# Batch loop of a two-layer mega-kernel written out: order of the batches, place of the experts, one projection run, and the shifted value rows by DMA from ScalarE's queue

## What is computed

```
x0  = x[b]                                  # (512, 128)
xn0 = layernorm(x0)
g   = minGRU(xn0) @ W2 + b2                 # log-space recurrence over tokens, width 256
h   = xn0
for l in 0, 1:                              # local attention, 8 heads of 64, window 64
    s = shift_token(h)                      # upper half of the channels one token later
    q, k, v = s @ wqkv[l]                   # q, k normalised, rotated
    h = h + local_softmax(q, k) @ v @ wo[l]
    h = h + mlp(layernorm(shift_token(h)))  # gelu gate, hidden 341
x1  = silu(h) * g + x0
xn1 = layernorm(x1)
o   = softmax(q1 k1^T, 16 heads of 16) v1 (heads of 64) @ wo1
out[b] = x1 + gate * o                      # gate: silu of the expert layer's result
```

## Time and profile before

| | |
|---|---|
| median of 3 runs | 3997.4 us (3994.64 to 4002.34) |
| the profiled execution's own time | 3996.54 us |
| its span (first to last instruction) | 3994.5 us |
| PE busy | 3230.1 us, 81% |
| DVE busy | 2735.6 us, 68% |
| ACT busy | 2412.9 us, 60% |
| POOL busy | 980.4 us, 25% |
| mean granted PE clock | 0.907 |

### The profile page before, as it was taken

One profiled execution on the slowest core, in us unless ns is written; L12 is line 12 of the kernel. 1 busy time (PEld: TensorE's weight loads), 2 busy tenths in 40 slices (PEclk: granted clock), 3 DMA queues, 4 the chain that ended last, 5 costly groups with the idle time before them and its releaser, 6 DMA issues.

```text
span 3994.5 us, 66851 instructions
## 1 busy us (share of the span) xinstructions
PE 3230.1 (81%) x20144; PEld 1629.3 (41%) x20144; DVE 2735.6 (68%) x4828; ACT 2412.9 (60%) x5081; POOL 980.4 (25%) x719
## 2 busy tenths in 40 slices
PE   4768788787878879787888878787887878788866
PEld 2445344444434444443434444343444444343411
DVE  3464486777767676777767677777767777786632
ACT  2344466666756666566766656675666667576543
POOL 1121121323222122322222132322212232232110
PEclk7679899898989989899998989999998989999876
DMA  2002001010010101001010101001010100101010
GB/s 65 1 4 67 20 20 49 19 49 15 16 51 20 47 20 47 13 30 37 21 47 20 47 20 41 19 20 51 19 48 16 51 13 23 44 17 47 20 50 19
DMA packets 112590, 124.19 MB, mean 31 GB/s; under 512 B 12435, under 2 KB 85693, under 8 KB 112189
## 3 DMA queue, kind: packets, MB, share of 16 engines
q1 hardware_dynamic: 112124, 119.26, 9.3%
q0 software_dynamic: 64, 0.01, 0.0%
HBM read 64.70 MB, written 54.53 MB: 30 GB/s over the span
## 4 chain that ended last, share of the span: by engine, by line
PE 55%; DVE 19%; issue 14%; ACT 6%; POOL 4%; DVEq 1%; SPq 1%; DMA 0%; POOLq 0%; ACTq 0%
PE pb L569 29%; PE o_bank L569 10%; PE s L569 7%; DVE nmax L1285 3%; PE y_bank L569 3%; PE pb L664 3%; PE pb L695 2%; POOL scratch L1370 2%; DVE stat L1179 2%; ACT ex L1017 2%; DVE stat L1209 2%; DVE scratch L1191 1%; PE pb L719 1%; DVE scratch L1192 1%; DVE mlp_h L1253 1%
## 5 line engine op out<-in xcount | busy, mean ns | idle before, releaser
L1017 ACT ACTIVATE ex<-s,nmax 128x512 f32<-128x512 f32 x1024 | 698.2, 684 | 510.4 <-DVE nmax L1285 485.2
L1285 DVE TENSOR_REDUCE nmax<-s 128x1 f32<-128x512 f32 x1024 | 684.4, 684 | 388.4 <-PE s L569 386.9
L1404 POOL TENSOR_TENSOR vsc<-vrow,rinv 128x256 f32<-128x256 f32 x256 | 172.9, 675 | 1755.0 <-DVE rinv L1293 1748.1
L569 PE MATMUL o_bank<-ex,vsc 128*64 128x512 f32 x2048 | 546.8, 658 | 69.2 <-POOL vsc L1404 55.7
L1365 POOL TENSOR_TENSOR scratch<-scratch 128x1024 f32<-128x1024 f32 x128 | 305.6, 2387 | 743.1 <-DVE scratch L1192 713.7
L569 PE MATMUL s<-qs,ks 96*128 96x512 bf16 x1024 | 387.8, 408 | 116.9 <-ACT ex L1017 72.3
L569 PE MATMUL pb<-wqkv,hsh 128*128 128x512 f32 x768 | 409.3, 654 | 43.6 <-ACT qT L951 22.1
L569 PE MATMUL pb<-kT,qT 64*64 64x64 f32 (+1 forms) x6144 | 333.3, 258 | 0.0
L664 PE MATMUL pb<-const,scratch 128*128 128x128 f32 x1024 | 174.1, 326 | 187.7 <-POOL scratch L1370 187.6
L569 PEld LDWEIGHTS pb<-kT,qT 64*64 64x64 f32 x6144 | 285.5, 145 | 87.5 <-issue 87.5
L954 ACT ACTIVATE scratch<-scratch 128x512 f32<-128x512 f32 x256 | 160.4, 627 | 256.8 <-DVE scratch L1213 256.8
(11 more groups left out here) (193 smaller groups left out, 6218.3 us busy)
## 6 DMA issues: line engine op xcount, KB each, us to landing
parts_store<-side SPq DMA_DIRECT2D x64, 384.0 KB, 2.6
qs<-parts_store SPq DMA_DIRECT2D x128, 192.0 KB, 2.8
ks<-parts_store SPq DMA_DIRECT2D x128, 192.0 KB, 3.1
parts_store<-side SPq DMA_DIRECT2D x64, 256.0 KB, 2.8
parts_store<-side SPq DMA_DIRECT2D x64, 128.0 KB, 2.6
xin<-in_L_attn_x SPq DMA_DIRECT2D x16, 256.0 KB, 3.5
ex<-in_L_ffn_w SPq DMA_DIRECT2D x16, 256.0 KB, 3.0
out<-yrow SPq DMA_DIRECT2D x16, 256.0 KB, 3.1
```

The source lines that it names most:

```text
L569: return pe.matmul(o, l, r, start=start, stop=stop, skip_group_check=True)
L1017: A(ex[:, w % 2, j, :], s_bank[c % 2][:], ACT.Exp, bias=nmax[:, c % 8:c % 8 + 1], accum_out=rsum[:, w % 2, j:j + 1]).then_inc(GA, 1)
L1285: V.tensor_reduce(nmax[:, c % 8:c % 8 + 1], s_bank[c % 2][:], X, ALU.max, negate=True).then_inc(GV, 1)
L1404: G.tensor_tensor(vsc[:, w % 2].rearrange("p (m a) d -> p m a d", a=2), vrow[:, m:m + 2, 2 * V1 * p:2 * V1 * (p + 1)].rearrange("p m (a d) ...
```

## The change

- The batch loop is written out: all of iterations -1 to 17 are straight code with constant semaphore values; `FRESH`, the registers and the table load at the loop head are gone.
- Batches are processed in the order 1, 2, ..., 15, 0. Position `b` loads and stores rows of batch `(b + 1) % B`.
- The experts become a fourth lane "x" with steps of its own, in iteration 16 only. Their weights have eight buffers laid over `qT`, `kT`, `va` and `vb`, all loaded by SP when the last local attention is over; the routing loads move to SP as well. The four adds of an expert start when all four of its tiles are there. Gelu of an expert is followed by a table load back.
- The projection is one step after the last pair (`o1T` has eight buffers), accumulated in `o_bank`; DVE does multiply and add in one instruction (two at the last position), POOL's part is gone.
- The copies to `vb` are DMAs issued from ACT, with a semaphore per tile; `pv` waits for it.
- All four `ORDER` strings are new.
- `dynamic_dma_scratch_size=1024` is given when the program is built.

```diff
-                s += {2: [("o", p)], 3: [("proj", p)]}.get(j, [])
+                s += {2: [("o", p)]}.get(j, [])
...
-    return values, s[:half], s[half:] + [("gate",), ("store",)]
+    return values, s[:half], s[half:] + [("proj",), ("gate",), ("store",)]
+def expert_steps():
+    s = [("route",)]
+    for e in range(E + 1):
+        if e < E:
+            s += [("h", e, j) for j in (1, 2, 3)]
+        if e:
+            s += [("t", e - 1, t) for t in range(NT)]
+        if e < E:
+            s += [("h", e, 0), ("gelu", e)]
+    return s + [("turn",), ("s1",), ("s2",), ("s3",), ("gated",)]
...
+        "x": lane("expert", -B, STEPS["expert"][:-1]),
...
-            steps(-1, merged(name))
-            steps(0, merged(name))
-            early = lambda x: x[0] in ("attn0", "post1", "keep0", "keep1") or x[2][0] == "values"
-            steps(1, [x for x in merged(name) if early(x)])
-            expert()
-            steps(1, [x for x in merged(name) if not early(x)])
-            with eng.Fori(2, B - 1) as i:
-                if name == "act":
-                    eng.preload_act_table_set(EXP_LN)
-                steps(i, merged(name))
-            for i in range(B - 1, B + 2):
-                steps(i, merged(name))
+            for i in range(-1, B + 2):
+                for flow, shift, s in merged(name):
+                    b = i + shift
+                    if name in MARKS[flow][s[0]] and (b == 0 if flow == "expert" else 0 <= b < B):
                         does[flow](b, s)
...
             def load_experts():
+                need(sp, attn[1], "dve", B - 1, ("wo", NT - 1), "x")
+                sp.dma_start(eidx, ...).then_inc(routing_loaded, 16)
+                sp.dma_start(ews, ...).then_inc(routing_loaded, 16)
                 for e in range(E):
+                    sp.dma_start(ew[e], a["L1_ffn_w1"][e]).then_inc(expert_loaded[e // 2], 16)
+                    sp.dma_start(ew2[e], ...).then_inc(expert_loaded[e // 2], 16)
...
+                    if par == 0:
+                        pe.wait_ge(vb_copied[t], (2 * b + l + 1) * (32 if t else 16))
...
                 elif kind == "proj":
+                    need(pe, glob, "act", b, ("o", H1 // 2 - 1), "t")
+                    for p in range(H1 // 2):
+                        last = mm(o_bank[:], wo1[:, p, :], o1T[:, p, :], start=(p == 0), stop=(p == H1 // 2 - 1))
+                    last.then_inc(GE, 1)
...
                     if t < NT - 1:
-                        A(vb[WIN:P, t + 1, :, 0:DH], va[WIN:P, t, :, 0:DH], ACT.Copy)
-                    A(vb[0:WIN, t, :, 0:DH], va[0:WIN, t, :, 0:DH], ACT.Copy).then_inc(FA, 1)
+                        act.dma_start(vb[WIN:P, t + 1], va[WIN:P, t]).then_inc(vb_copied[t + 1], 16)
+                    act.dma_start(vb[0:WIN, t], va[0:WIN, t]).then_inc(vb_copied[t], 16)
...
                 elif kind == "gate":
+                    if b == B - 1:
+                        V.tensor_tensor(yf, o_bank[:], es[3], ALU.mult).then_inc(expert.sem["dve"], 1)
+                        dve.wait_ge(expert.sem["dve"], expert.count("dve", 0, ("gated",), "y"))
+                        V.tensor_tensor(yf, yf, x1[:], ALU.add).then_inc(GV, 1)
+                    else:
+                        V.scalar_tensor_tensor(yf, o_bank[:], gate1, x1[:], ALU.mult, ALU.add).then_inc(GV, 1)
```

More of the change, by code:

```diff
@@ L205 @@
     "proj": {"pe": ["y"]},
-    "gate": {"dve": ["g"], "pool": ["x", "g"]},
+    "gate": {"dve": ["x"]},
     "store": {"pe": ["t"], "act": ["t"]},
+}
+EXPERT_MARKS = {
+    "route": {"dve": ["i", *(f"w{e}" for e in range(E)), "w"]},
+    "h": {"pe": ["p"]},
+    "gelu": {"act": [f"g{j}" for j in range(JF)]},
+    "t": {"pe": ["p"], "dve": ["a"]},
+    "turn": {"pe": ["t"]},
+    "s1": {"dve": ["b", "m"], "act": ["e", "l"]},
+    "s2": {"dve": ["d"], "act": ["s"]},
+    "s3": {"dve": ["g"]},
+    "gated": {"dve": ["y"]},
 }
@@ L304, in build @@
         flows = {name: Flow(name, sem) for name in STEPS}
-        pre, gru, glob, keep0, keep1 = (flows[n] for n in ("pre", "gru", "glob", "keep0", "keep1"))
+        pre, gru, glob, keep0, keep1, expert = (
+            flows[n] for n in ("pre", "gru", "glob", "keep0", "keep1", "expert"))
         attn, post = (flows["attn0"], flows["attn1"]), (flows["post0"], flows["post1"])
@@ L371, in build @@
         vsc = sb("vsc", [P, 2, 4, V1])
-        o1T = sb("o1T", [P, N])
-        x1, gate, yf, yrow = (sb(n, [P, N])[:] for n in ("x1", "gate", "yf", "yrow"))
+        o1T = sb("o1T", [P, H1 // 2, N])
+        x1 = sb("x1", [P, N])
+        yf, yrow = o1T[:, 6, :], o1T[:, 7, :]
         store = nc.dram_tensor("parts_store", [B, 2, 2, len(Q_PART), K1, H1 // 2, N], BF16, kind="Internal").ap()
@@ L386, in build @@
         s_bank = [bank("s0"), bank("s1")]
-        o_bank, y_bank = bank("o_bank"), bank("y_bank")
+        o_bank, warm_bank = bank("o_bank"), bank("warm")
         token_rows = a["L0_attn_x"].rearrange("b (t p) d -> b p t d", p=P)
@@ L518, in _ @@
             load_x(0)
-            step(0)
-            step(1)
-            with sp.Fori(2, B - 1) as i:
-                step(i)
-            for i in range(B - 1, B + 2):
+            for i in range(B + 2):
                 step(i)
@@ L527, in _, with run @@
                 sp.wait_ge(p, 2 * PUT_COUNT * B)
-        def run(eng, name, does, expert):
+        def run(eng, name, does):
             for f in flows.values():
@@ L1028, in glob_does @@
-                    A(yrow[:], y_bank[:], ACT.Copy).then_inc(GA, 1)
-            def expert():
-                for e in range(E):
-                    for j in range(JF):
-                        act.wait_ge(expert_pe, 8 * e + j + 1)
-                        if e:
-                            act.wait_ge(expert_pe, 8 * e)
-                        A(eh[:, j, :], pb[:, j, :], ACT.Gelu).then_inc(expert_act, 1)
-                act.preload_act_table_set(EXP_LN)
-                act.wait_ge(expert_dve, E * NT + 2)
-                A(es[2], es[1], ACT.Exp).then_inc(expert_act, 1)
-                act.wait_ge(expert_act, E * JF + 1)
-                A(es[2], es[2], ACT.Ln, bias=1.0).then_inc(expert_act, 1)
-                act.wait_ge(expert_dve, E * NT + 3)
-                A(es[3], es[3], ACT.Exp).then_inc(expert_act, 1)
+                    A(yrow, o_bank[:], ACT.Copy).then_inc(GA, 1)
@@ L1130, in gru_does @@
                     need(dve, gru, "pe", b, s, "p")
-                    if j == 0 and not (isinstance(b, int) and b == 0):
+                    if j == 0 and b:
                         for p in parts_stored:
```

253 lines of the change are left out of this document (127 added, 126 removed).

## The result

The changed kernel takes 3930.2 us (median of 4, 3929.6 to 3931.3): 0.9829 of the kernel before, which took 3998.8 us beside it (median of 4), 95% interval 0.9812 to 0.9846. That is 68 us less where I forecast 141. The direction and the range held, the size did not, and few terms of the sum agree with what was measured.

The account below looks back on a forecast made before the run. No engine was full (PE nearest, 84% busy in the loop); lanes waiting for each other bound it. 3996.5 - 81 - 64 - 71 + 75 = 3855.5, or 3856 us against the median; range 3750 to 3935.

Parts of the forecast that it names:

- Parts 2 to 4: vb DMAs, one-run projection and new orders together: -4 us a batch, -64 us over 16 batches, bounds +32 and -220.
- iterations above 224: Sign named beforehand that would show the forecast wrong; it expected iterations of about 218 us.
- One run, "-2 a batch": Projection in one run: shorter PE waits for the o1T copies, -2 us a batch; matmul pairs moved at no cost.
- DMAs, "-2": vb copies as DMAs issued by ACT at 0.32 us each: ACT gains 4.3 us, -2 us a batch on the path.
- New orders, "0": New lane orders: taken as 0, sign unknown; bounds up to 6 us an iteration worse, or 206 us an iteration.
- Part 1: Loop written out: 6.2 us less an iteration, -81 us over 13 iterations, bounds -42 and -99.
- Part 5: Experts taken out of iteration 1, where they ran alone for 78.5 us: -71 us, bounds -70 and -78.5.
- Part 6: Experts put into iteration 16, half beside the tail's heads, half running alone: +75 us, range 44 to 118.
- Better packed: Rival: the new orders pack better, 208 us an iteration instead of 218, so 3716 us; chance 0.15.
- ACT's issues block: Rival: each vb DMA issue holds ACT's sequencer 1.215 us, so slower, 4019 us; chance 0.05.
- Only the back edge goes: Rival: writing the loop out gains only the loop edges, 42 us, so 3959 us; chance 0.15.
- The tail is dearer: Rival: experts 0 to 3 add 32 us, lone experts and projection run at low clock: +38, 3894 us; chance 0.15.

Follow-up runs that it names:

- e2: b1 with the first seven of eight projection matmuls cut from 512 to 2 columns; 3918.8 us, timed once.
- b1: Kernel before, loop written out and experts moved to iteration 16; old order, single projections and ACT's copies kept; 3890.0 us, ratio 0.973.
- f3: b1 with experts 4 to 7 moved beside heads 8 to 15 of the last batch, plus five idle matmuls of only two columns; 3885.9 us, timed once.
- a5: Changed kernel without its expert layer and routing, every gate the constant column; 3897.1 us, timed once.
- u1_written_out: Kernel before with its batch loop written out as straight code, nothing else; 3914.2 us, ratio 0.979.
- a3: Changed kernel with the old order and the vb copies back on ACT, projection still in one run; 4023.4 us, ratio 1.006.
- a2: Changed kernel with the old interleaving of lanes a, s and g; 4009.9 us, ratio 1.003.
- f1: Changed kernel plus eight idle matmuls an iteration in front of PE's longest waits; 3870.2 us, ratio 0.968.

## Why the prediction came out as it did

**What a us at 1.2 GHz costs.** I compare iterations of one kernel against each other: 217.9 us with 13.7 at 1.2 GHz and 225.2 with 34.1 (e2); 220.7 with 17.1 and 223.1 with 23.9 (b1); 221.8 with 20.5 and 225.3 with 30.7 (f3); 225.2 with 30.7 and 228.7 with 41.0 (a5). That is 0.36, 0.35, 0.34 and 0.34 us for each: a third and a bit. I use 0.35 to compare kernels at an equal clock. It is a slope within kernels, so I take what it leaves over between kernels as good to about 1 us, which is an estimate.

**The step that failed** is "Parts 2 to 4 together are -4 a batch, 16 batches: **-64 us**". They came to +3.4 us an iteration (221.85 to 225.27), +50 us from u1_written_out to the changed kernel over all stages before the tail but the experts'. That is 114 us of error, which other terms made smaller: 40 us of the other sign in Parts 1, 5 and 6. That 3930.2 still lies in the range is luck, not a sum that held. The prediction's own sign of being wrong, iterations above 224, came with 225.3. Along one path of kernels the +3.4 us are: +0.2 from u1 to b1, +8.0 for the run (b1 to a3), -0.8 for the DMAs (a3 to a2) and -3.9 for the orders (a2 to the changed kernel). By its pieces:

- *Clock, which no term had:* 23.6 to 30.7 us at 1.2 GHz, x 0.35 = +2.5 of the +3.4. I read the clock in the loop, 0.94, as a constant. It moved with every piece of the change, between 21.0 and 52.0 us at 1.2 GHz an iteration, and work put into or taken out of PE's waits moved it (f1 and e2).
- *One run, "-2 a batch":* +8.0 in the old order, of which clock 10.2 x 0.35 = 3.6, and 4.4 the run itself. That the matmul pairs are "moved, not removed" is true. To cost the move at nothing was the error. Single pairs stood in time in which PE would have waited: cutting seven of them saves, at an equal clock, 9.5 x 0.35 - 1.6 = 1.7 us of their 6.5. Cutting them out of the run saves 5.5 + 1.9 x 0.35 = 6.2. Moving them into one piece put 4.5 us on the path. The gain was to come from the waits for `o1T`. In b1 they are 71.6 us and in a3 17.0, and a3 is the slower one: their going gained nothing that can be seen. In the loop of the kernel before they were small, 2.1 us an iteration, most of it weight loads (first fence below).
- *DMAs, "-2":* +1.9 and +1.5 in the old order with single projections, -0.8 with the run, -3.4 in the new order. At an equal clock these are -0.2, +0.4, -0.2 and -1.2, against the 1.1 us that ACT really gains. In the old order the loss that one sees is the clock's. Two readings failed. The issue price is 0.55 us on average by the medians, not 0.32. And the 2.0 us a batch of PE waiting for these copies are not in the loop: of the ten waits seven lie in iterations 0 and 1 and three behind the loop, none in its 13 iterations (second fence below). Why the DMAs shift the clock is not settled.
- *New orders, "0":* between -3.4 and -4.4 at an equal clock with the one run, +12 with single projections. A sign could not be had from the trace of before. What came for the orders as they were adopted lies within the bounds; the +12 belongs to a kernel that the forecast was not about.

```profile
  PEld y_bank L569: 23.8, 39
  PE y_bank L569: 4.0, 13
```
```profile
  PEld pb L664: 19.9, 4
...
  PEld pb L664: 8.7, 3
...
  PEld pb L664: 3.9, 3
```

Both are of the kernel before: who waited for tile `o1T` between 564.4 and 3531.4 us, and who waited for line L938 until 271.2 us, from there to 564.4 us, and from 3531.4 us on (us, times). Between 564.4 and 3531.4 us the view of L938 lists nobody.

**Right: Part 1.** -81 forecast; u1_written_out against before -83.7 over the whole span. Of the 6.4 us an iteration, 4.8 x 0.35 = 1.7 are again clock.

**Right in kind: Part 5.** Iteration 1 fell by 83.4 us, where 71 were forecast, and lies outside the bounds of 70 to 78.5. In the old order with single projections it is 80.0 (293.1 in u1, 213.1 in b1). So nothing came back of the 7.5 us that I had kept for `values` of batch 0, and some 3 us are of the new steps. Iteration 1 before and after:

```profile
271.20:564.40 293.20, 230.58 (x1442) 130.80 (x1442) 164.25 (x302) 146.84 (x280) 56.21 (x35) 0.90 0.11 33
...
272.50:482.20 209.70, 163.55 (x1102) 89.56 (x1112) 145.50 (x255) 114.37 (x228) 51.63 (x33) 0.89 0.12 35
```

**Mis-sized: Part 6.** It is +50.4 against u1_written_out for a forecast of +75. The stages against the kernel before, whose tail is 0.5 us shorter than u1's: Projection and route (+7): that stage is 12.7 us *shorter*, 75.7 at a clock of 0.95 for 88.4 at 0.83. This isn't the experts' doing, since without them it is 76.6 (a5_noexpert). Experts 0 to 3 (+15): +3.1. Heads 8 to 15 (0): -2.5. Last projection and gate (+9): +6.8. Experts 4 to 7 (+44): 56.3. Their cycle is 13.9 us, not 9.6; the timeline shows why:

```profile
3798.36 1.13 DVE L1337 SCALAR_TENSOR_TENSOR scratch<-pb,scratch 128x128 f32<-128x128 f32 x4 [11.72 <-PE pb L572]
3799.54 1.13 PE L572 MATMUL pb<-xn,kT 128*128 128x512 f32 x2 [1.29 <-DVE scratch L1337]
3800.75 1.28 ACT L1043 ACT_TABLE_LOAD   x1 [8.59 <-PE pb L572]
3802.04 2.06 ACT L1043 ACTIVATE scratch<-pb 128x512 f32<-128x512 f32 x4
3803.27 5.29 PE L572 MATMUL pb<-xn,kT 128*128 128x512 f32 x6 [2.60 <-ACT scratch L1043]
...
3808.40 3.73 PE L572 MATMUL pb<-vb,scratch 128*128 128x128 f32 x32
```

Everything happens one after the other: the adds, PE's matmul into the bank that they read, ACT's table load that starts only when its first input is there, 1.28 us, the Gelus, and PE at a clock of 0.74 in between.

**The sum** with what was measured: 3996.5 - 83.7 (loop) + 50.2 (Parts 2 to 4) - 83.4 + 50.4 = 3930.0; the profiled execution took 3929.9. It must come out, since the terms are differences of the same traces.

**The rivals.** "Better packed" was wrong in the iteration. "ACT's issues block" was wrong: no issue is above 0.721 us. "Only the back edge goes" was wrong: the written-out loop alone gained twice the edges' 42 us. "The tail is dearer" was half right, in the lone experts, and wrong in the sum. What did happen, that the new steps make the iteration longer than a plain written-out one, was in the words "above 224" but in no case of its own.

**The version that beats both.** Loop written out, experts split over the last two iterations, single projections, old order, ACT's copies and five idle matmuls: 3828.7 us, 0.9578 of the time before (0.9561 to 0.9594), 2.6% under the changed kernel.

## What to carry to other kernels

Take a multi-part change apart before it is adopted: here the loop written out alone beat all of it together. Work that stands in an engine's waits costs little; collected into one piece it costs nearly its whole time. Before a wait is counted as a gain, look in which stage it lies. When TensorE waits several us in the middle of a busy loop, look at the granted clock behind the wait, and try idle matmuls in it.

## What the runs showed of the hardware

- Leaving out 6.5 us of matmul made an iteration 1.6 us longer (one execution), and adding 7.4 us made it 3.7 us shorter. The time at 1.2 GHz went from 21.0 to 30.5 us and from 30.7 to 10.5 us.
- Iterations with the same instructions take one of a few lengths, 217.9 or 225.4, 225.2 or 228.7, and keep or alternate them for hundreds of us. A difference of 1 to 3 us an iteration between two kernels can be this alone.
- A DMA from SBUF to SBUF of 64 rows, issued by ACT, holds its sequencer 0.47 to 0.61 us, against 0.62 for the copy that it replaces, and lands after 2.3 us.
